# A graph network on one core: the first edge pass gets a ring of eight gathered groups instead of four

## The reference, cut to what matters

```
h = max(layernorm(x), 0)
x = x + conv2(relu(conv1(h)))        # mean over edges of h[src], times W_nbr; plus h @ W_root + b
h = max(layernorm(x), 0)
z = concat(h[src], h[dst], edge_attr) @ W.T + b        # 256 columns, one row for each edge
z = batchnorm over the edges (z)
x = x + scatter_add(by src, sigmoid(z[:, :128]) * softplus(z[:, 128:]))
```

## Time and profile before

| | us |
|---|---|
| median of three runs | 4759.76 (4754.23 to 4768.53) |
| the profiled execution, its own time | 4766.37 |
| its span, first to last instruction | 4764.4 |

### The profile page before, as it was taken

How to read it: one execution, slowest core, us unless ns; L and a number is a source line. 1 busy time by engine, 2 the same in 40 slices (tenths; PEclk the granted TensorE clock), 3 DMA queues, 4 the chain that set the end, 5 groups by cost and what they waited for, 6 DMA issues and landing times.

```text
span 4764.4 us, 74664 instructions
## 1 busy us (share of the span) xinstructions
PE 3037.7 (64%) x16593; PEld 2074.8 (44%) x16717; DVE 1924.3 (40%) x4127; ACT 1412.4 (30%) x2638; POOL 2539.8 (53%) x2543
## 2 busy tenths in 40 slices
PE   1777677757878886788888888862121235555366
PEld 1455455544555554455555555531111124444255
DVE  6444444454444456422222222333232334454355
ACT  3222222220000001321121221227677754454500
POOL 4455554544655551466666666547777764454600
PEclk9787787768887887899999999985555557777599
DMA  3222222222222221577777777754444444545343
GB/s 96 72 63 78 75 74 64 90 68 78 87 84 85 84 83 32 182 231 232 239 229 234 230 228 233 226 190 147 135 140 135 146 132 134 162 139 168 106 100 102
DMA packets 360456, 645.05 MB, mean 135 GB/s; under 512 B 62184, under 2 KB 226380, under 8 KB 355216
## 3 DMA queue, kind: packets, MB, share of 16 engines
q1 hardware_dynamic: 264016, 392.92, 26.0%
q0 software_dynamic: 93440, 218.82, 15.5%
q10 hardware_dynamic: 2880, 32.11, 1.9%
HBM read 439.34 MB, written 204.28 MB: 135 GB/s over the span
## 4 chain that ended last, share of the span: by engine, by line
PE 37%; issue 19%; another core or an unknown queue 14%; ACT 10%; DVE 9%; DVEq 8%; DMA 2%; ACTq 0%; SPq 0%; POOL 0%; POOLq 0%
PE PS L1644 6%; PE PS L1489 6%; PE PS L1638 5%; PE PS L1629 5%; PE PS L1479 5%; PE PS L1661 4%; ACT arena L940 2%; DMA Q<-z_tab 2%; DVEq L383 2%; DVEq L1069 1%; PE PS L1475 1%; ACT Q L935 1%; DVEq L1360 1%; PE PS L1550 1%
## 5 line engine op out<-in xcount | busy, mean ns | idle before, releaser
L725 POOL DMA_INDIRECT Q<-h_tab,src_i x960 | 943.8, 983 | 804.8 <-PE PS L1556 361.6
L752 POOL DMA_INDIRECT m_tab<-Q,pos_i x784 | 834.1, 1064 | 492.8 <-ACT Q L959 265.8
L725 POOL DMA_INDIRECT arena<-p_tab,src_i x784 | 743.6, 949 | 617.7 <-issue 213.8
L1671 PE MATMUL PS<-ident,arena 128*128 128x128 f32 x784 | 203.5, 410 | 808.6 <-DVE arena L1386 426.6
L1489 PE MATMUL PS<-Q 128*128 x2684 | 490.2, 337 | 178.1 <-DVE Q L1071 81.8
L1302 DVE BATCH_NORM_STATS2 stats<-arena 128x512 f32 (+1 forms) x392 | 251.5, 684 | 712.3 <-ACT arena L920 688.2
L1489 PEld LDWEIGHTS PS<-Q 128*128 128x128 f32 x2684 | 419.8, 237 | 272.6 <-issue 268.3
L920 ACT ACTIVATE arena<-PS,LB 128x512 f32<-128x512 f32 x392 | 243.2, 686 | 993.1 <-remote 859.9
L1671 PEld LDWEIGHTS PS<-ident,arena 128*128 128x128 f32 x784 | 131.2, 205 | 869.3 <-issue 714.9
L1661 PE MATMUL PS<-Q 128*128 x2336 | 400.5, 328 | 154.2 <-issue 77.2
L1661 PEld LDWEIGHTS PS<-Q 128*128 128x128 f32 x2336 | 349.4, 230 | 209.3 <-issue 207.1
(11 more groups left out here) (219 smaller groups left out, 4026.9 us busy)
## 6 DMA issues: line engine op xcount, KB each, us to landing
z_tab<-arena SPq DMA_DIRECT2D x196, 512.0 KB
Q<-z_tab SPq DMA_DIRECT2D x196, 512.0 KB
Q<-m_tab SPq DMA_DIRECT2D x196, 264.0 KB
arena<-in_edge_t SPq DMA_DIRECT2D x196, 256.0 KB
arena<-dst_tab SPq DMA_DIRECT2D x196, 128.0 KB
count_tab<-Q SPq DMA_DIRECT2D x11, 1568.0 KB
Q<-count_tab ACTq DMA_DIRECT2D x10, 1568.0 KB
arena<-count_tab ACTq DMA_DIRECT2D x10, 1568.0 KB
```

What stands on the lines that cost most here:

```text
L725: nc.gpsimd.indirect_dma_start(buf[:, s * GT + k, 0:width], None, table, bass.IndirectOffsetOnAxis(src_i[:, t:t + 1], 0)).then_inc(landed[ ...
L752: nc.gpsimd.indirect_dma_start(m_tab, bass.IndirectOffsetOnAxis(pos_i[:, t:t + 1], 0), mrow[:, s, k, :], None).then_inc(ms.scattered[s], 16)
L1671: ins = turn(PS[:, 2 + q, t * P:(t + 1) * P], msg_t[:, q, t * P:(t + 1) * P], ident[:])
```

## The change

The P rows get a ring of `RP` = 8 groups. Groups 4 to 7 of each eight are gathered into `H`, which is free once `X` holds the sum of both. So the additions of H to X move from the pass to the end of the node stage, as seven additions of seven tiles each, and POOL waits for them (`p1.x_merged`) ahead of group 4. The semaphores `rows_landed` become eight instead of six. The convs still use six of them, in the same way. TensorE's loop over the pass is written out for eight groups in each turn (24 turns and four groups behind them), with the same instructions in each group. Everything else keeps four slots: PSUM, edge data, z buffers.

```
+    RP = 8
...
+        prow_h, _ = carve(H[:].rearrange("p a b -> p (a b)"), 0, SL * GT, H2)
...
+        def conv_row(s, k):
+            return rows[:, s * GT + k, 0:F]
+
+        def p_row(s, k):
+            return (prow_h if s >= SL else prow_a)[:, s % SL * GT + k, :]
...
-        rows_landed = ring("rows_landed", CS)
+        rows_landed = ring("rows_landed", RP)
...
                 depth = len(landed)
                 for g in range(first, NG):
                     s = (g - first) % depth
+                    if table is p_tab and g == SL:
+                        pool.wait_ge(p1.x_merged, NI)
                     if g >= first + depth:
                         pool.wait_ge(freed, before + g - first - depth + 1)
...
-            gather_all(p_tab, prow, H2, p1.done, SL, rows_landed[0:SL], 0)
+            gather_all(p_tab, p_row, p1.done, SL, rows_landed, 0)
...
             for c in range(len(SUBS) * (NI - 2), CH + 1):
                 rests(c)
+            for i in range(NI):
+                v.tensor_tensor(node_tiles(X, i), node_tiles(X, i), node_tiles(H, i), ALU.add).then_inc(p1.x_merged, 1)
...
-                if s == SL - 1 and not (isinstance(i, int) and i == ITER):
-                    x = X[:, ds(i, 1), :].rearrange("p a f -> p (a f)")
-                    v.tensor_tensor(x, x, H[:, ds(i, 1), :].rearrange("p a f -> p (a f)"), ALU.add)
...
-            with pe.Fori(0, ITER) as i:
-                for s in range(SL):
-                    g = i * SL + s
+            def pass1(t, u):
+                s, turn = u % SL, t * (RP // SL) + u // SL
+                g = t * RP + u
...
+                pe.wait_ge(rows_landed[u], t * (16 * GT) + 16 * GT * ((2 * CITER if u < CS else 0) + 1))
+                for k in range(GT):
+                    for h in range(2):
+                        ins = mm(PS[:, 2 * s + h, k * P:(k + 1) * P],
+                                 p_row(u, k)[:, h * F:(h + 1) * F], ident[:], start=False, stop=k == GT - 1,
+                                 skip_group_check=True)
+                ins.then_inc(p1.done, 1)
+            with pe.Fori(0, NG // RP) as t:
+                for u in range(RP):
+                    pass1(t, u)
+            for u in range(NG % RP):
+                pass1(NG // RP, u)
```

More of the change, by code:

```diff
@@ L161, in build_gnn @@
         ht, a = carve(arena, a, 2, NB * F)
-        prow, a = carve(arena, 0, SL * GT, H2)
+        prow_a, a = carve(arena, 0, SL * GT, H2)
         ebuf, a = carve(arena, a, SL, GE)
@@ L352, in build_gnn @@
         p1.oht_ready, p1.oht_used, p1.z_ready = sem("pass1_oht_ready"), sem("pass1_oht_used"), sem("pass1_z_ready")
+        p1.x_merged = sem("pass1_x_merged")
         p1.done, p1.stats_done = sem("pass1_done"), sem("pass1_stats_done")
@@ L713, in _, with gather_all @@
             nc.gpsimd.memset(AGG, 0.0).then_inc(agg_zeroed, 1)
-            def gather_all(table, buf, width, freed, before, landed, first):
+            def gather_all(table, row, freed, before, landed, first):
                 depth = len(landed)
@@ L724, in gather_all @@
                         t = g * GT + k
-                        nc.gpsimd.indirect_dma_start(buf[:, s * GT + k, 0:width], None, table,
+                        nc.gpsimd.indirect_dma_start(row(s, k), None, table,
                                                      bass.IndirectOffsetOnAxis(src_i[:, t:t + 1], 0)
@@ L730, in _ @@
             pool.wait_ge(ln.stored, 16 * NI)
-            gather_all(h_tab[0], rows, F, conv[0].group_done, 0, rows_landed, DG)
+            gather_all(h_tab[0], conv_row, conv[0].group_done, 0, rows_landed[0:CS], DG)
             pool.wait_ge(node[0].h_ready, NI)
@@ L734, in _ @@
             pool.wait_ge(node[0].stored, 16 * NI)
-            gather_all(h_tab[1], rows, F, conv[1].group_done, CITER * CS, rows_landed, DG)
+            gather_all(h_tab[1], conv_row, conv[1].group_done, CITER * CS, rows_landed[0:CS], DG)
             all_stored(pool, pq.p_stored)
-            gather_all(p_tab, prow, H2, p1.done, SL, rows_landed[0:SL], 0)
+            gather_all(p_tab, p_row, p1.done, SL, rows_landed, 0)
             pool.wait_ge(p1.done, NG + SL)
@@ L1621, in _ @@
             pe.reg_mov(pair, 0)
-            with pe.Fori(0, ITER) as i:
-                for s in range(SL):
-                    g = i * SL + s
-                    lo, hi = windows(pe, g)
-                    pe.wait_ge(p1.edges_landed[s], i * 32 + 32)
-                    pe.wait_ge(p1.z_ready, g + 1)
-                    for h in range(2):
[L1629 to L1645, removed]
-                                     skip_group_check=True)
-                    ins.then_inc(p1.done, 1)
@@ new lines, in pass1 @@
+            def pass1(t, u):
+                s, turn = u % SL, t * (RP // SL) + u // SL
+                g = t * RP + u
+                lo, hi = windows(pe, g)
+                pe.wait_ge(p1.edges_landed[s], turn * 32 + 32)
+                pe.wait_ge(p1.z_ready, g + 1)
+                for h in range(2):
+                    mm(PS[:, 2 * s + h, :], WC[:, h * F:(h + 1) * F], ebuf[:, s, :], start=True, stop=False,
+                       skip_group_check=True)
+                with pe.Fori(lo, hi) as w:
+                    m, w = tick(pe, pair), window(w)
+                    pe.wait_ge(p1.oht_ready, m)
+                    hot = oht[:, ds(m % 2, 1), :].rearrange("p a e -> p (a e)")
+                    for h in range(2):
+                        for j in range(3):
+                            part = Q[:, j, ds(w, 1), h * F:(h + 1) * F].rearrange("p a b -> p (a b)")
+                            ins = mm(PS[:, 2 * s + h, :], part, hot, start=False, stop=False,
+                                     skip_group_check=True)
+                    ins.then_inc(p1.oht_used, 1)
+                pe.wait_ge(rows_landed[u], t * (16 * GT) + 16 * GT * ((2 * CITER if u < CS else 0) + 1))
+                for k in range(GT):
+                    for h in range(2):
+                        ins = mm(PS[:, 2 * s + h, k * P:(k + 1) * P],
+                                 p_row(u, k)[:, h * F:(h + 1) * F], ident[:], start=False, stop=k == GT - 1,
+                                 skip_group_check=True)
+                ins.then_inc(p1.done, 1)
```

## The result

The changed kernel takes 4774.02 us (median of 15 runs, 4764.91 to 4791.0), the kernel before, timed beside it, 4760.29 us (15 runs, 4754.23 to 4768.53). The ratio is 1.0030, with a 95% interval of 1.0019 to 1.0041. So the change makes the kernel 13.7 us slower, and the interval does not reach down to 1. The forecast was 4773 us, and the range 4745 to 4800. In a second set of runs (`after_2`) the ratio was 1.0039 (1.0025 to 1.0053).

A forecast was written before the change was run, and what follows sets the result against it. The prediction took gathers holding PE's signals, closing a two-group loop, as the bound. Terms 0 + 16.7 - 3.5 - 1 + 1 = +13.2 gave 4779.6 us profiled; the median, 6.6 us lower, 4773 us; range 4745 to 4800.

The forecast's parts named there:

- The reading: In the pass, a signal PE gives during back-to-back gathers arrives only when the row ends: 5.4 and 10.4 us late.
- The middle of the pass: Mid-pass: POOL again waits for PE's signals group by group, so 6.15 us a group stay; 0 us.
- Rival A: Pass: the ring uncouples POOL and PE, 5.12 us a group, 4555 us, chance 0.14; weak form -15 to -60, 0.06.
- The first fill: Pass start: 32 gathers instead of 16, 20.0 us more, less 3.3 us of PE's work while crawling; +16.7 us.
- Rival C: First fill: group 0's signal slips through, POOL adds groups 8 and 9, PE stays held; 4787 us, chance 0.13.
- Rival B: First fill: the longer row of gathers holds nobody, only the ends count; -3.5 us, 4756 us, chance 0.17.
- The end: Pass end: POOL finishes four groups earlier, so PE runs the last groups without gathers; -3.5 us.
- Additions out of the pass: Pass: 13.5 us of VectorE additions leave it, which matters only where a one-hot is late; -1 us.
- The additions at the new place: End of node stage: seven additions, 7.6 us, mostly hidden; first gathers beside them may slow, 0 to +5, taken +1 us.
- PE's loop of eight groups: PE's pass loop: same instructions a group, twice the code a turn, half the turns; 0 us, bounds ±5.

The follow-up runs named there:

- Credit 4: The changed kernel with POOL's credit in the pass limited to four groups: 4762.8 us, ratio 0.9990 to the kernel before.
- 6 groups of credit: The changed kernel with POOL's credit in the pass limited to six groups: 4767.33 us, ratio 1.0001 to the kernel before.
- ramp: The changed kernel with credit growing one group each 40 groups, from four to eight: 4116.31 us beside a kernel before of 4112.28 us, 1.0013.
- credit 3: The changed kernel with POOL's credit in the pass limited to three groups: 4759.71 us, ratio 0.9986 to the kernel before.

## Why the prediction was right, and where it was not

*The reading.* That the gathers hold PE's signals is shown, by taking the gathers away (5.12 us a group with either kind of plain transfer). "Only when the row of gathers is over" was too strict. A signal that is given early in a row gets through, and the trace of before had it: the group whose transposes end at 2511.12, 1.6 us into the row of eight, is taken up at once.

```profile
2511.32 1.26 ACT L920 ACTIVATE arena<-PS,LB 128x512 f32<-128x512 f32 x2 [1.23 <-PE PS L1644]
```

That the hold belongs to the kernel on every chip is not so either: on one of the three chips of the experiments it didn't happen.

The Trainium skill ("SBUF — State Buffer", "Who interferes with whom") has it that DMA never contends with a compute engine. The plain transfers agree with it (PE at 5.12 us a group beside the same bytes), the gathers don't on the chips of the first kind (6.15 us a group).

*The middle of the pass, 0.* Right: 131 gathers in 200 us against 130, and 324 activations in 1000 us against 322. Rival A falls in the sense that matters for this change. POOL and PE are coupled, and 5.12 us a group are to be had, but with credits of 3 to 8 groups the long middle (groups 12 to 180) stayed at 6.19 to 6.23 us a group.

*The first fill, +16.7.* Right in kind, too small in size. Credit 4 is the fair measure, as it differs from the change in the depth alone: group 12 comes at 115.0 us with 8 groups and at 92.8 with 4, so +22.2. Of the two terms of the forecast the 20.0 us of sixteen more gathers held: the row is 47.1 us against 27.0, +20.1. The other, 3.3 us back for what PE gets done while crawling, was mis-sized: in the last 20 us of the row PE did 8 instructions, where the forecast had 13 (26 with their weight loads), and none of it shows in group 12's time. And a term was missing, the stop behind the row, which grew from 4.00 to 6.26 us, +2.3. Together +22.4, where group 12 shows +22.2.

*The signal that slipped through.* Rival C said "none slipped in 10.4 us here". In the changed kernel group 0's signal did, as in every kernel with the additions moved on chips of the first kind (first rows of 36, 28, 20 and 16 gathers for credits of 8, 6, 4 and 3; before, 16 for 4). The additions slow the first three gathers. When group 0's transposes end, 8 gathers have begun in the changed kernel (1947.74 + 1.95 = 1949.69) and 10 in the one before (1960.88); ScalarE follows after 2.9 and after 10.4 us. So the moved additions are a likely reason, which no run here isolates; the number of gathers begun is not the whole rule, as in mid-pass the signal of 2515.92 is held with 6 begun in its row. The slip costs next to nothing: a fifth group of gathers adds 5.0 us to credit 4's row, but three groups are done at its end and not two (6.15 us), and group 12 comes at 92.8 us where it was 92.5. Of rival C's chain only this first link came true: group 8 was added, group 9 was not.

By the marks that the prediction gave: the first activation before 1980 us was to speak for B, and it did come early, at 1952.60, but for one group alone, and the second, at 1990.59, is where the forecast had the first (near 1991). The first row of more than 32 gathers was to speak for C, and does.

*The end, -3.5.* The last 15 groups (180 to 195) took 82.9 us, against 88.9 before and 86.0 with credit 4. That would make the ring's part -3.1, as forecast. But it is a difference of single profiles, and with 6 groups of credit the same stretch took 90.7 us. From group 12 to the end, where such shifts within the pass cancel, it is 1133.2 us with 3 groups, 1131.2 with 4, 1129.8 with 6, and 1128.2 and 1125.9 with 8. So the direction is as forecast, and the size -3 to -5 us against credit 4, as far as single profiles tell.

*Additions out of the pass, -1.* Here the size isn't settled. Credit 4 differs from before by the additions' place and the long loop alone: group 12 at 92.8 us (92.5 before), from there to group 180 1045.2 us (1051.0), then 86.0 (88.9): -8.4 us in the pass, by one profile of each. The other four kernels with the additions moved that ran on chips of the first kind took 1039.1 to 1046.3 us for the middle part, all below 1051.0, of which there is one profile only. The times of the whole kernel say a ratio of 0.9990, -4.8 us (-10.5 to +1.0), and that interval holds both the forecast and no gain at all.

*The sum.* In the profiled executions: +22.5 - 5.6 - 6.0 = +10.9 for the pass, forecast +13.2. The ring alone, change against credit 4: +22.2 + 0.2 - 3.1 = +19.3 us, and +16.9 with `after_2`'s profile; by the ratios (1.0030 less 0.9990, from separate sets of runs) 0.40%, 19 us as well; forecast 16.7 - 3.5 = +13.2. In these profiles the ring costs 4 to 6 us more than forecast and the moved additions give about as much more. That the time was hit to 1 us is luck: the two errors cancel. The sign and the stage are not.

*The additions at the new place, +1.* They took 7.10 us from 1936.82, the first row above (forecast 7.6). Three gathers beside them took 1.70 to 1.72 us, 2.3 us more in all, which lies between the 0 and +5 and above the +1 taken. The Trainium skill ("SBUF — State Buffer", "Who interferes with whom") has a VectorE instruction with two SBUF inputs contend with a GpSimd one that reads SBUF. The trace agrees: 1.70 us beside the additions, 0.95 us behind them. PE waited for rows for 0.4 us in all. Group 0's second one-hot (1944.92 + 0.35) was ready before PE's use of it at 1945.70, as forecast.

*PE's loop of eight groups, 0.* Right within what was measured: credit 4, which has it together with the moved additions, is level with before.

*Rival B* (the fill holds nobody) fell on this kind of chip: ScalarE waited 36.72 us. It is what happens on the other kind, where the same change in its credit-ramp form was within 0.3%.

Open: what makes one chip different; which part of a gather holds PE and SyncE; and from where in a row on a signal is held.

## What to carry to other kernels

Before giving a queue more credit, look in the trace at who waits for whom. Here the consumer never waited for rows; a deeper ring gave 3 to 5 us at the end, and each group of credit above four put off group 12 by 5.5 us. Where POOL's waits and ScalarE's end together and "remote" (a releaser that the profile can't name), try plain transfers in place of the gathers first: one run shows what the gathers really cost (220 us here), and that a change should aim at their number before their buffers, which is a conclusion and was not tried. The loss here depends on the chip too, so compare only with a kernel timed beside it.

## What the runs showed of the hardware that was not expected

- One of the three chips of the experiments does not hold PE's signals beside gathers. The unchanged kernel takes 4112.28 us there (17 runs) and 4753.96 to 4765.02 us on the others, so 14% less, with gathers of the same 0.95 us and a mean PE clock of 0.824 (`ramp`'s profile) against 0.800 (before's).
- The stop after a row of gathers grows with the row: 2.67 us after 8, 3.68 after 16 (3.50 with credit 3), 4.00 after 20, 5.08 after 28, 6.26 after 36. That is (6.26 - 2.67) / 28 = 0.13 us for each gather on top of about 1.6 us, as if the work that a gather leaves behind took 0.13 us longer than the 1.251 us in which the next one is issued, and the signals stood behind it. This is a reading of five numbers, not shown by itself; after eight gathers a rest of 1.56 us was in fact shorter than the 1.93 us that the signal took.
- Late in a long row PE issues one transpose instruction each 2.1 to 2.8 us (up to 2.52 us idle ahead of one of 0.37 us), though the profile names nothing that it waits for. PE's first such stop in the pass comes 16.8 us after the first gather in the kernel before (1965.34) and 19.3 us after it in the changed one (1957.31), both times with 14 gathers begun. SyncE's two reloads, 0.52 us apart otherwise, are 1.46 to 1.96 us apart in a row.
